# Decoder block on one core: VectorE's low parts set between its additions, the second norm's work spread anew, GpSimd's powers behind the next weights' sums

## What is computed

```
x = x + attn(layernorm(x))                 # one head of 128, with its projection out
x = x + xattn(layernorm(x), ctx)           # 32 heads of 128, rmsnorm with a weight inside, mask and position bias
x = x + ffn(layernorm(x))                  # 512x512 product plus top-2 of 8 low-rank experts

def xattn(h, ctx):                         # the part that this change is about
    n  = rmsnorm(h, ln_weight)
    hq = (n   @ w_q.T)                     # 1024 tokens x 512 -> 32 heads x 128
    hk = (ctx @ w_k.T)
    hv = (ctx @ w_v.T)
    p  = softmax(where(mask, hq @ hk.T + bias, -inf))
    return h + (p @ hv) @ w_out.T
```

## Time and profile before

| | |
|---|---|
| median of three runs | 885.33 us (884.88 to 886.03) |
| the profiled execution, its time | 887.64 us |
| its span | 885.9 us |
| granted clock of TensorE, mean over the span | 0.99 |
| TensorE busy | 848.4 us, 96% |
| VectorE busy | 639.6 us, 72% |
| ScalarE busy | 409.0 us, 46% |
| GpSimd busy | 358.7 us, 40% |
| DMA over the span | 158 GB/s |

### The profile page before, as it was taken

How to read it: one execution, slowest core, us unless ns; L and a number is a source line. 1 busy time by engine, 2 the same in 40 slices (tenths; PEclk the granted TensorE clock), 3 DMA queues, 4 the chain that set the end, 5 groups by cost and what they waited for, 6 DMA issues and landing times.

```text
span 885.9 us, 14164 instructions
## 1 busy us (share of the span) xinstructions
PE 848.4 (96%) x4288; PEld 709.3 (80%) x4288; DVE 639.6 (72%) x1116; ACT 409.0 (46%) x1064; POOL 358.7 (40%) x331
## 2 busy tenths in 40 slices
PE   5789998999999999999999999999999999999898
PEld 4677776887777788787888888888888888888797
DVE  7877776567887766657788777886667866677654
ACT  3453443565433453355455544555345553454220
POOL 2312324223443432235554666545564455643000
PEclk9899999999999999999999999999999999999999
DMA  8026575555666567746777756766566765772002
GB/s 284 2 86 149 136 168 139 142 143 128 169 144 164 142 157 166 143 110 193 219 222 224 204 173 203 197 199 200 171 204 193 202 192 179 205 200 62 1 1 95
DMA packets 231281, 139.78 MB, mean 158 GB/s; under 512 B 139216, under 2 KB 205904, under 8 KB 229328
## 3 DMA queue, kind: packets, MB, share of 16 engines
q1 hardware_dynamic: 231248, 139.38, 57.8%
HBM read 90.07 MB, written 49.28 MB: 157 GB/s over the span
## 4 chain that ended last, share of the span: by engine, by line
PE 81%; DVE 10%; issue 2%; POOL 2%; DMA 2%; ACT 1%; SPq 1%; DVEq 0%; ACTq 0%; POOLq 0%
PE bank L650 66%; PE bank L704 7%; PE bank L789 6%; DVE w_lo L1399 2%; DVE turned L1491 2%; DVE st L1408 1%; DMA values<-turned 1%; PE bank L668 1%; SPq L353 1%; DMA raw_a<-in_w_qkv 1%; POOL w_sum L538 1%; POOL rstd L517 1%; DVE stats L1277 1%; POOL w_sum L536 1%; ACT st L1065 0%
## 5 line engine op out<-in xcount | busy, mean ns | idle before, releaser
L1065 ACT COPY st<-bank 128x512 f32<-128x512 f32 x192 | 112.6, 587 | 245.5 <-PE bank L650 244.6
L650 PE MATMUL bank<-ctx_hi,w_hi 128*128 128x512 f32 x448 | 180.4, 403 | 15.5 <-DVE st L1408 7.4
L650 PE MATMUL bank<-ctx_lo,w_hi 128*128 128x512 f32 x448 | 175.7, 392 | 0.0
L650 PE MATMUL bank<-ctx_hi,w_lo 128*128 128x512 f32 x448 | 175.6, 392 | 0.0
L1408 DVE TENSOR_TENSOR st<-bank,st 128x512 f32<-128x512 f32 x144 | 98.5, 689 | 95.8 <-PE bank L650 95.6
L536 POOL TENSOR_TENSOR w_sum<-raw 128x256 f32<-128x256 f32 x48 | 39.5, 824 | 248.4 <-PE bank L650 226.6
L604 POOL TENSOR_TENSOR weighed<-probs,row_scale 128x512 f32<-128x512 f32 x64 | 70.5, 1107 | 126.4 <-DVE row_scale L1360 125.8
L650 PEld LDWEIGHTS bank<-ctx_hi,w_hi 128*128 128x128 f32 x448 | 84.7, 189 | 45.4 <-issue 10.6
L1011 ACT ACTIVATE probs<-probs,neg_max 128x128 f32<-128x128 f32 x264 | 102.4, 391 | 5.9 <-DVE neg_max L1344 5.9
L1399 DVE TENSOR_TENSOR w_lo<-w_sum,w_hi 128x512 fp32r<-128x512 f32 x96 | 81.8, 862 | 25.3 <-POOL w_sum L544 19.9
L650 PEld LDWEIGHTS bank<-ctx_hi,w_lo 128*128 128x128 f32 x448 | 84.8, 189 | 18.3
(11 more groups left out here) (148 smaller groups left out, 1507.9 us busy)
## 6 DMA issues: line engine op xcount, KB each, us to landing
raw<-in_weights SPq DMA_DIRECT2D x128, 256.0 KB, 3.6
values<-turned SPq DMA_DIRECT2D x64, 256.0 KB, 4.3
v<-values SPq DMA_DIRECT2D x64, 256.0 KB, 4.8
by_blocks<-probs SPq DMA_DIRECT2D x30, 512.0 KB, 3.2
probs_t<-by_blocks SPq DMA_DIRECT2D x120, 128.0 KB, 2.8
keys<-st SPq DMA_DIRECT2D x14, 1024.0 KB, 5.2
st<-keys SPq DMA_DIRECT2D x28, 512.0 KB, 5.6
acc<-in_x SPq DMA_DIRECT2D x8, 256.0 KB, 6.0
```

Source lines behind the costliest of these rows:

```text
L650: ins = pe.matmul(out_ap, lhs[a], rhs[b], start=start and k == 0, stop=stop and k == n - 1, skip_group_check=again)
L1065: act.copy(to[:, i, j, :], (y, other, y, y)[which][:, :]).then_inc(act_took, 1)
```

## The change

Three edits. (1) GpSimd: the two `root` calls of the second norm stand behind the sums for projection 10, not behind those for projection 9. (2) VectorE: of the four low parts, two stay ahead of the first addition, the third goes between the first and second addition, and the fourth between the second and third, in all projections from 2 to 31. (3) The extra work of the second norm is distributed anew over the projections, in the VectorE and the ScalarE table; on VectorE almost all of it now hangs behind even projections. The unrolled part of ScalarE's and VectorE's loops grows accordingly (to 9 and 12 groups).

```diff
@@ gpsimd
             for n in range(2, 22):
                 sum_for(n)
-                if n == 9:
+                if n == 10:
                     root(1, half(0), spans(1, 0))
                     root(1, half(1), spans(1, 1))
@@ scalar
             beside = {9: lambda: rows_high(0), 10: lambda: rows_high(1), 11: lambda: take_rows(0),
-                      12: lambda: take_rows(1), 13: lambda: x_highs(0, 3), 14: lambda: x_highs(5, 1),
-                      15: lambda: x_highs(4), 16: lambda: x_highs(2), 17: lambda: x_highs(6)}
-            for k in range(1, 9):
+                      12: lambda: take_rows(1), 13: lambda: x_highs(0, 3), 14: lambda: x_highs(5),
+                      15: lambda: x_highs(1), 17: lambda: x_highs(4), 18: lambda: x_highs(2), 19: lambda: x_highs(6)}
+            for k in range(1, 10):
...
@@ vector
-            def lows(p, m):
-                for part in range(4):
-                    low(p, m, part)
-
-            def takes(n, of, odd=False):
-                for which in range(3):
-                    take(n, which, st[of], odd)
+            def takes(n, of, p, m, odd=False):
+                low(p, m, 0)
+                low(p, m, 1)
+                take(n, 0, st[of], odd)
+                low(p, m, 2)
+                take(n, 1, st[of], odd)
+                low(p, m, 3)
+                take(n, 2, st[of], odd)
...
-            beside = {2: lambda: add_b_o(0, 1), 3: lambda: add_b_o(2, 3, 4, 5), 4: lambda: add_b_o(6, 7),
-                      5: lambda: own_stats(0, 1, 2), 6: lambda: own_stats(3), 7: lambda: own_stats(4, 5, 6, 7),
-                      8: both_spreads, 11: lambda: add_normalised(0), 13: lambda: x_sum(0, 1, 2),
-                      14: lambda: x_sum(3), 15: lambda: add_normalised(1), 16: lambda: masks(0),
-                      17: lambda: x_lows(0, 3), 18: lambda: masks(1), 19: lambda: x_lows(5, 1), 20: lambda: x_lows(4),
-                      21: lambda: x_lows(2, 6)}
-            for k in range(1, 11):
+            beside = {2: lambda: add_b_o(0, 1), 3: lambda: add_b_o(2), 4: lambda: add_b_o(3, 4, 5, 6),
+                      5: lambda: add_b_o(7), 6: lambda: own_stats(0, 1, 2, 3, 4), 7: lambda: own_stats(5),
+                      10: lambda: add_normalised(0), 12: lambda: add_normalised(1), 14: lambda: x_sum(0, 1),
+                      18: lambda: x_lows(0, 3), 20: lambda: x_lows(5, 1), 24: lambda: x_lows(2, 6)}
+            for k in range(1, 13):
                 for n, taken in ((2 * k, keys_taken), (2 * k + 1, values_taken)):
                     taken(k)
                     if n in beside:
                         beside[n]()
+                    elif n == 8:
+                        own_stats(6, 7)
+                        both_spreads()
+                    elif n == 16:
+                        masks(0)
+                        x_sum(2, 3)
+                    elif n == 22:
+                        x_lows(4)
+                        masks(1)
...
             turn(V1 - 1, GROUPS - 3, 1)
-            lows(1, V0 // 2)
-            takes(V1, 0)
+            takes(V1, 0, 1, V0 // 2)
...
```

More of the change, by code:

```diff
@@ L1146, in _ @@
             beside = {9: lambda: rows_high(0), 10: lambda: rows_high(1), 11: lambda: take_rows(0),
-                      12: lambda: take_rows(1), 13: lambda: x_highs(0, 3), 14: lambda: x_highs(5, 1),
-                      15: lambda: x_highs(4), 16: lambda: x_highs(2), 17: lambda: x_highs(6)}
-            for k in range(1, 9):
+                      12: lambda: take_rows(1), 13: lambda: x_highs(0, 3), 14: lambda: x_highs(5),
+                      15: lambda: x_highs(1), 17: lambda: x_highs(4), 18: lambda: x_highs(2), 19: lambda: x_highs(6)}
+            for k in range(1, 10):
                 keys_taken(k, beside.get(2 * k))
                 values_taken(k, beside.get(2 * k + 1))
-            with act.Fori(9, GROUPS - 2) as k:
+            with act.Fori(10, GROUPS - 2) as k:
                 keys_taken(k)
@@ L1506, in turn @@
                 turn_blocks(of, 1, 0)
-            def lows(p, m):
-                for part in range(4):
-                    low(p, m, part)
-            def takes(n, of, odd=False):
-                for which in range(3):
-                    take(n, which, st[of], odd)
+            def takes(n, of, p, m, odd=False):
[6 more added lines that the diff above has]
+                take(n, 2, st[of], odd)
             def keys_taken(k):
                 turn(2 * k - 1, k - 1, 1)
-                lows(1, k)
-                takes(2 * k, 0)
+                takes(2 * k, 0, 1, k)
             def values_taken(k):
-                lows(0, k + 1)
-                takes(2 * k + 1, 1, odd=True)
+                takes(2 * k + 1, 1, 0, k + 1, odd=True)
             def add_b_o(*some):
@@ L1575, in _ @@
                         beside[n]()
-            with dve.Fori(11, GROUPS - 2) as k:
+                    elif n == 8:
[7 more added lines that the diff above has]
+                        masks(1)
+            with dve.Fori(13, GROUPS - 2) as k:
                 keys_taken(k)
@@ L1579, in _ @@
             turn(V1 - 1, GROUPS - 3, 1)
-            lows(1, V0 // 2)
-            takes(V1, 0)
+            takes(V1, 0, 1, V0 // 2)
             turn(V1, GROUPS - 2, 0)
-            lows(0, K0 // 2)
-            takes(V0, 1, odd=True)
+            takes(V0, 1, 0, K0 // 2, odd=True)
             turn(V0, GROUPS - 1, 1)
[L1586 to L1589, removed]
+            takes(K0, 0, 1, Q0 // 2)
+            takes(Q0, 1, 0, K1 // 2, odd=True)
             def low_for_queries(g, part):
```

## The result

| | before | after |
|---|---|---|
| median of the first comparison, four runs each | 885.68 us (884.88 to 886.25) | 871.44 us (868.82 to 873.25) |
| ratio, 95% interval | | 0.9838, 0.9806 to 0.9869 |
| two more comparisons (15 and 11 runs before, five each after) | 886.74 and 885.95 | 867.95 and 868.37 |
| their ratios | | 0.9792, 0.977 to 0.9814; 0.9804, 0.9785 to 0.9822 |
| profiled execution: time, span | 887.64, 885.9 | 868.82, 867.1 |

The change makes the kernel faster. The median forecast was 867.0 (864.3 to 872.5), the profiled execution's forecast 869.3 with a span of 867.6. Fourteen executions of the changed kernel were timed in all: twelve lie between 867.52 and 869.91, two at 872.97 and 873.25.

A forecast was written before the change was run, and what follows sets the result against it. TensorE, busy 848.4 us, was taken as the bound, with gains only from its idle time and slowed matmuls. 16.8 plus 1.8 less 0.3 gave 18.3 us off the 885.33 median: 867.0 us, range 864.3 to 872.5.

The forecast's parts named there:

- The sum: Projects 3 to 23 gain 16.8 us, those outside 1.8, less 0.3 for queues: 18.3 us gained.
- the 0.3 for queues: Crowded DMA from later raw-weight loads: cost 0, bounds 0 and 0.3 us; 0.3 was taken off the gain.
- the forecast's case: Main outcome around 867.0 us, including unchanged quiet projects or no loss in 17 and 19: 864.5 to 870.5, chance 0.80.
- late powers: Rival: GpSimd's sums stretch, so ScalarE's rows and TensorE's turning slip 2 to 3 us: 869.5 to 870, chance 0.12.
- Part 1, the powers: Project 9: GpSimd's sums for project 10 go ahead of the second norm's powers; removes 6.6 us, margin 0.9.
- Part 2, the alternation: VectorE's low parts between additions: quiet projects go from 9.62 to 9.53 us, with 0.07 to spare at the tightest place.
- half-gain rival: Low parts between additions come late wherever there is extra work, so only project 9 is mended: 878.7 us, chance 0.06.
- Part 3, placement: Second norm's extra work redistributed over projects: VectorE's own lateness goes, some GpSimd lateness stays.
- GpSimd's lateness beside extra work: GpSimd's sums held up by VectorE's extra work: 0.2 us each in projects 15, 19, 21 and 25, 0.9 in 17.
- the 0.9 us for the mask additions: Low part behind GpSimd's mask addition delays the second addition: 0.5 us in project 17, 0.4 in 19; bounds 0 and 2.5.
- the slower rival: Raw-weight loads issued later land too late, stopping GpSimd, ScalarE, VectorE and TensorE in turn: 889 us, chance 0.02.
- Projection 30: Turned tiles wait for stored values; with two low parts behind them the first addition is on time: 1.1 us gained.

The follow-up runs named there:

- experiment 2: Kernel before with only GpSimd's powers moved behind the sums for project 10: 880.56 us, ratio 0.9928.
- experiment 5: Kernel before with the powers moved and the low parts set between the additions, second norm's work in its old placement: 869.65 us, ratio 0.9816.
- experiment 10: Changed kernel with one more power, its result unused, between GpSimd's sums for project 10 and the second norm's powers: 871.06 us, ratio 0.9847 to the kernel before.
- experiment 4: Changed kernel with GpSimd's powers back in front of the sums for project 10: 875.26 us, ratio 0.9874 to the kernel before.
- experiment 3: Kernel before with only two of VectorE's four low parts set between the additions in projects 2 to 31: 873.76 us, ratio 0.9863.
- experiment 6: Changed kernel with all four low parts in front of the first addition again: 882.0 us, ratio 0.9957 to the kernel before.
- experiment 9: Changed kernel with raw-weight loads held back until three slots of the next projection are done: 870.53 us, ratio 0.9855 to the kernel before.

## Why the prediction was right, point by point

**The sum.** The stretch gave 18.27 us for 18.3, and from projection 3 to 23 it was 206.27 for 206.0. Behind the close match stand errors that cancel: the losses in odd projections were 0.4 us larger in 3 to 23 than the 2.4 forecast and 0.2 larger in 25, and projections 10 and 12 took 9.62; against that a quiet projection takes 9.52 and not 9.53, the turnings cost 1.67 each in place of 1.75, and the 0.3 for queues did not come. The profiled execution's 868.82 stands beside 869.3.

**The median** came out at 871.44, 4.4 above 867.0; the two later ones are 867.95 and 868.37. The step from the sum to the median took the 18.3 us off 885.33, and this median of three runs is on the low side: the comparisons have 885.68, 886.74 and 885.95 for the kernel before. 18.3 less than these is 867.4, 868.4 and 867.7, so the gain between medians came out as forecast within 0.5 and 0.7 us in the two later comparisons, and was 4.0 short in the first, where two of four executions are near 873. These two had a mean granted clock of 0.990 and 0.988, the other twelve 0.994 to 0.998, and the slowest execution of the kernel before in any comparison, 894.71 us, had 0.987. The two weren't profiled: where their clock fell, and whether that was the cause, is not shown. The range of 864.3 to 872.5 holds 871.44, though the forecast's case with its own 864.5 to 870.5 doesn't; the range's top was meant for late powers, which did not come, so that it covered this scatter is luck.

What the prediction had no term for is that the rest of the kernel doesn't stand still. This window of the opening is of before (columns as in the window above):

```profile
22.00:44.00 22.00, 17.38 (x83) 14.13 (x83) 17.69 (x22) 10.90 (x23) 8.50 (x7) 0.84 0.00 1
```

After:

```profile
22.00:44.00 22.00, 18.19 (x92) 14.85 (x91) 18.83 (x23) 12.10 (x26) 8.83 (x8) 0.92 0.02 5
```

Of the twelve traces, eight have 0.92 there, and their projection 2 starts at 73.90 to 74.47 us; four have 0.84 (before, and experiments 2, 5 and 10), with 74.83 to 76.67. What comes behind projection 33 takes 483.0 to 486.7 us. So executions differ by some us outside the stretch of the change, whatever the edit, and part of that goes with the opening's clock.

**Part 1, the powers.** Right in its gain: 6.4 us alone (experiment 2), 6.6 forecast. Mis-sized was the moment at which the spreads are ready: S+3.4, not S+2.1. Without sums beside them it would have been right: in experiment 4 they are ready at S+1.97. VectorE runs the same operations twice, for half 0 beside GpSimd's sums and for half 1 beside its powers:

```profile
144.36 0.67 DVE L1298 TENSOR_SCALAR spread<-spread 128x4 f32<-128x4 f32 x1
...
146.02 0.17 DVE L1298 TENSOR_SCALAR spread<-spread 128x4 f32<-128x4 f32 x1
```

Three such operations of half 0 were drawn out from 0.16 or 0.17 to between 0.63 and 0.72 us, 1.5 us together. The sums hid that. Half 0 was raised by S+5.9 (5.6 forecast), the rows were done at S+8.9 (8.6), 0.63 us before the turning (0.9), and of that 0.46 could be used, as experiment 10 measures. The late-powers rival is thereby out in this kernel, but close: a single power more made it true. It is also the part on which the changed placement leans, as experiment 4 shows (8.3 us if it is taken back).

**Part 2, the alternation.** Right and the largest: 12.4 us alone (experiment 3) where I expected 10.5 by then, 13.3 when it is taken out of the changed kernel (experiment 6). The 0.07 us to spare held in every quiet projection; no low part between the additions waited for a high part of ScalarE's (those in front of the first addition sometimes did, at no cost). The half-gain rival (878.7) is refuted by this, as is its reason.

**Part 3, placement.** The claim that VectorE's own lateness goes came true, but experiment 5 shows that the alternation alone had already removed it: the same stretch without the placement. I had given placement a share in the 10.7 us that don't belong to projection 9; its share is 0.1 us at most against the first trace. The 1.3 us between the two medians (869.65 and 868.37) aren't the stretch's: in the two traces the opening is 0.8 longer and the rest 0.7, while the stretch is 0.5 shorter. And the placement isn't neutral by itself: with all low parts in front it costs 1.4 us (experiment 6 against 2).

**GpSimd's lateness beside extra work** was mis-sized twice, in opposite senses. First, two 128x1024 operations ahead of an odd projection cost 0.41 us, not 0.2, and four bias additions in front of projection 5 cost 0.41, not 0: a GpSimd sum ran for 1.60 us instead of 0.74 beside the first kind and for 0.92 to 1.09 beside the second, and what reached TensorE was a row of short restarts: in projection 15 slots 2, 3 and 4 took 1.41, 1.57 and 1.49 us in place of 1.36 each, without a line in the view of waits. Second, the 0.9 us for the mask additions did not come. GpSimd, ScalarE, TensorE and VectorE in projection 17 (S = 221.71):

```profile
221.95 1.61 POOL L536 TENSOR_TENSOR w_sum<-raw 128x256 f32<-128x256 f32 x1 [6.19 <-PE bank L650]
223.64 1.60 POOL L538 TENSOR_TENSOR w_sum<-w_sum,raw 128x256 f32<-128x256 f32 x1
225.27 0.62 ACT L1057 CAST w_hi<-w_sum 128x512 fp32r<-128x512 f32 x1 [1.42 <-POOL w_sum L538]
226.43 0.50 PE L650 MATMUL bank<-ctx_hi,w_hi 128*128 128x512 f32 x1 [0.48 <-ACT st L1065]
226.76 2.87 POOL L561 TENSOR_TENSOR bias_mask<-mask_add,bias 128x1024 f32<-128x1024 f32 x1
228.13 0.69 DVE L1408 TENSOR_TENSOR st<-bank,st 128x512 f32<-128x512 f32 x1 [0.77 <-PE bank L650]
228.74 1.44 DVE L1399 TENSOR_TENSOR w_lo<-w_sum,w_hi 128x512 fp32r<-128x512 f32 x1
230.10 0.68 DVE L1408 TENSOR_TENSOR st<-bank,st 128x512 f32<-128x512 f32 x1
230.84 0.48 PE L650 MATMUL bank<-ctx_hi,w_hi 128*128 128x512 f32 x1
```

Read it in order: two sums of 1.6 us beside two subtractions, a high part that waits 1.42 for the second of them, a copy behind that, and TensorE starts slot 3 at S+4.72 instead of 4.08. That is 0.64 of the 1.09 us lost; slots 3 and 4 took 1.57 and 1.49, another 0.34. The mask addition followed the sums at once, from S+5.05 (I had put a low part between them, and 5.8), and ended at S+7.92, not 8.2. The low part in its shadow waited for it, as forecast, and took 1.44 us; the second addition came behind it at 230.10 = S+8.39, not 8.75. It could have run from 229.78, 0.29 after slot 5's first matmul. So it was 0.32 late, just inside the 0.38 us of slack: slot 6 is released just in time, its first matmul is drawn out to 0.48 us (the last row), and it takes 1.48. The mask addition thus cost 0.12 us here and 0.09 in projection 19 (slot 6 of 1.45), in place of 0.5 and 0.4. Near such a cushion a third of a microsecond in the estimate decides between all and nothing. Altogether projection 17 lost 1.09 (1.4 forecast), 19 lost 0.50 (0.6).

The Trainium skill ("SBUF — State Buffer", Who interferes with whom) calls this an exclusive lock between a VectorE operation with two SBUF inputs and GpSimd. The runs agree for the sums and the mask addition: the additions, with one input in PSUM, stayed at 0.69 us beside every GpSimd operation, the low part in front of them stretched from 0.69 to 1.44 and the sums from 0.74 to 1.6. The page frees an instruction with one SBUF input only outside VectorE's two-port modes, which the prediction left out; the forecast doesn't hang on it. For GpSimd's powers the runs do not agree with a lock that holds for the whole instruction: in projection 9 a low part with two SBUF inputs ran for its usual 0.68 us inside a power's 1.64 (durations on GpSimd are rough in a profile, but this one covers the low part by 0.4 us on either side).

```profile
147.41 1.64 POOL L517 TENSOR_TENSOR rstd<-spread,minus_half 128x8 f32<-128x8 f32 x1
147.86 0.68 DVE L1399 TENSOR_TENSOR w_lo<-w_sum,w_hi 128x512 fp32r<-128x512 f32 x1
```

**Queues and the slower rival.** The loads are issued at S+8.3 in quiet projections (8.4 forecast) and at S+8.7 in projection 25 (S = 299.87), in this row of SyncE's issues, against S+6.1 in the earlier trace rows:

```profile
308.58 1.21 SPq L318 DMA_DIRECT2D raw<-in_weights  x2
```

The changed kernel paid nothing for them, and 5.5 us more of lateness cost at most 1.8 us in all (experiment 9), so 889 was far off. The rival's mechanism was wrong too: first to give at that delay is ScalarE's wait for the stored keys, not GpSimd's for the weights.

**Projection 30** was right in two of three traces, 9.52 us for 9.53 (10.05 in the third). In the first, the tiles are turned from 349.96 to 352.45 (S+4.6) after 2.55 us of waiting for stored values, and the first addition runs at 353.51 = S+5.64:

```profile
349.96 2.49 DVE L1491 STREAM_TRANSPOSE turned<-st 128x512 f32<-128x512 f32 x4 [2.55 <-DMA values<-turned]
...
353.51 0.69 DVE L1408 TENSOR_TENSOR st<-bank,st 128x512 f32<-128x512 f32 x1 [0.15 <-PE bank L650]
```

## What to carry to other kernels

In an engine's program order, put just in front of an operation with a deadline only what that deadline needs, and set the rest into the gaps between deadlines; here that order gave 12.4 us. With it in, moving the extra work to other projections was worth 0.1 us at most; moving it *inside* the projections, in smaller shares, was worth 2.8, and which of the two does it was not tried apart. Price a change over the stretch on which it acts, cut out of the trace at two instructions, and allow a couple of us either way for what the rest does by itself; take the base from more than three runs. When several delays follow one another on a path, count each against the engine as late as it already is, or one lateness is paid twice.

## What the hardware showed that I had not expected

- A late release that the waits' view doesn't list still costs. With a release just in time the slot's first matmul takes 0.47 to 0.50 us in place of 0.39, and the slot some 0.1 to 0.2 us more (projection 5 after the change: slots 4 and 5 of 1.49 and 1.38 us behind a slot 3 of 1.62, together 0.41). A drawn-out first matmul alone doesn't prove a late release, though: the first one behind a turning took 0.48 us too (projections 10 and 12 after the change), 2.1 us after VectorE's last addition of the projection before had ended.
- VectorE's small operations are hit by GpSimd too: beside GpSimd's sums three of those on the 128x4 spreads took 0.63 to 0.72 us instead of 0.16 or 0.17. Two of the three have a single SBUF input. Beside GpSimd's powers the same three kept their 0.16 or 0.17 us.
- The granted clock of the opening (22 to 44 us) was 0.84 or 0.92 from one execution to the next though no edit touches that stretch, and the start of projection 2 moved with it, by up to 2.8 us.
